# Two-layer convolution and sparse-coding kernel: the normalisation statistics go through TensorE once instead of twice, and the work is put in another order

## The reference

```python
def _gn(v, G=32, eps=1e-5):            # two channels form a group
    g = v.reshape(B_, G, C_ // G, H_, W_)
    m = jnp.mean(g, axis=(2, 3, 4), keepdims=True)
    s = jnp.var(g, axis=(2, 3, 4), keepdims=True)
    return ((g - m) / jnp.sqrt(s + eps)).reshape(v.shape)

x = x + _L0_conv_ref(_gn(x), L0_conv_weight)       # 3 x 3 convolution, circular
x = x + _L1_conv_ref(_gn(x), L1_conv_dictionary)   # sparse coding of 4 x 4 patches
```

## Time and profile before

| | us |
|---|---|
| median of 3 runs | 3585.17 |
| lowest, highest | 3581.29, 3589.22 |
| profiled execution | 3581.48 |
| its span (first to last instruction) | 3579.5 |
| PE busy | 3067.3 (86%) |
| DVE busy | 2579.2 (72%) |
| ACT busy | 2367.6 (66%) |
| POOL busy | 1856.7 (52%) |

### The profile page before, as it was taken

The page is one execution under the profiler, slowest core; times in us unless marked ns, Lnnn a source line. Parts: engine busy times, 40 slices in busy tenths (PEclk is TensorE's granted clock), DMA queues, the critical chain, the costliest instruction groups (busy, mean ns, idle before and its releaser), DMA issues.

```text
span 3579.5 us, 35041 instructions
## 1 busy us (share of the span) xinstructions
PE 3067.3 (86%) x9488; PEld 1310.8 (37%) x9488; DVE 2579.2 (72%) x6596; ACT 2367.6 (66%) x3795; POOL 1856.7 (52%) x1861
## 2 busy tenths in 40 slices
PE   6796889899898989989898989989898998986617
PEld 2232333343333334333333434333333433332303
DVE  2027887878788687878778786878778777887872
ACT  3535686858677676858668685767768576765634
POOL 0015565555555564655656555555655555556651
PEclk8998999999999989999999999999999999997858
DMA  3433443534354343434444353445435344442222
GB/s 114 154 108 117 136 132 97 180 84 145 102 163 132 124 139 91 156 91 154 133 141 131 101 177 73 151 114 158 127 109 163 86 144 102 127 106 60 59 59 47
DMA packets 131028, 428.38 MB, mean 120 GB/s; under 512 B 55696, under 2 KB 55952, under 8 KB 106128
## 3 DMA queue, kind: packets, MB, share of 16 engines
q0 software_dynamic: 91136, 202.10, 23.3%
q1 hardware_dynamic: 39696, 224.05, 17.1%
HBM read 289.70 MB, written 136.31 MB: 119 GB/s over the span
## 4 chain that ended last, share of the span: by engine, by line
PE 49%; DVE 15%; issue 10%; ACT 10%; POOL 8%; DMA 5%; ACTq 0%; POOLq 0%; SPq 0%; DVEq 0%
PE gen_ps L909 22%; PE gen_ps L918 15%; PE conv_ps L952 8%; POOL v L479 7%; DVE u L832 6%; ACT hot L543 4%; PE conv_ps L959 4%; DMA u<-marked_rows,chosen 4%; DVE idx L732 2%; DVE h L840 2%; DVE top L723 2%; ACT score L617 1%; ACT junk_sums L356 1%; ACT ct L530 1%; ACT z L567 1%
## 5 line engine op out<-in xcount | busy, mean ns | idle before, releaser
L479 POOL DMA_INDIRECT v<-gram_rows,cell x1280 | 1278.2, 999 | 919.3 <-DVE cell L741 392.4
L909 PE MATMUL gen_ps<-ct,dt 128*128 128x512 f32 x2048 | 948.1, 618 | 69.6 <-ACT rb L555 60.3
L918 PE MATMUL gen_ps<-dn,z 128*128 128x512 f32 x2048 | 927.9, 607 | 62.4 <-ACT z L567 50.8
L952 PE MATMUL conv_ps<-xh,wc 128*128 128x512 f32 x1536 | 717.1, 617 | 91.0 <-ACT xa L585 83.5
L491 POOL DMA_INDIRECT u<-marked_rows,chosen x504 | 506.1, 1004 | 492.8 <-DVE chosen L737 329.0
L723 DVE MAX8 top<-score 128x8 f32<-128x512 f32 x640 | 420.7, 691 | 294.6 <-ACT score L617 278.5
L909 PEld LDWEIGHTS gen_ps<-ct,dt 128*128 128x128 f32 x2048 | 400.5, 198 | 583.2 <-issue 571.2
L918 PEld LDWEIGHTS gen_ps<-dn,z 128*128 128x128 f32 x2048 | 389.9, 194 | 568.0 <-issue 512.9
L832 DVE SCALAR_TENSOR_TENSOR u<-u,nl 128x512 f32<-128x512 f32 x748 | 514.2, 747 | 95.4 <-DMA u<-marked_rows,chosen 92.6
L617 ACT ACTIVATE score<-h 128x512 f32<-128x512 f32 x640 | 377.6, 604 | 241.3 <-DVE h L840 120.4
L655 DVE SCALAR_TENSOR_TENSOR ce<-hot,xc,ce 128x512 f32<-128x512 f16 x512 | 365.1, 745 | 159.1 <-ACT hot L546 159.1
(11 more groups left out here) (103 smaller groups left out, 1870.5 us busy)
## 6 DMA issues: line engine op xcount, KB each, us to landing
xh<-x_paired SPq DMA_DIRECT2D x128, 650.0 KB, 4.0
xa<-x_pairs SPq DMA_DIRECT2D x64, 1024.0 KB, 6.1
y_rows<-xa SPq DMA_DIRECT2D x64, 1024.0 KB, 6.3
y_rows<-rb POOLq DMA_DIRECT2D x64, 1024.0 KB, 8.3
v<-gram_rows,cell POOLq DMA_INDIRECT x1280
u<-marked_rows,chosen POOLq DMA_INDIRECT x504, 3.8
dn<-atoms SPq DMA_DIRECT2D x1, 2048.0 KB, 7.8
gram_rows<-u SPq DMA_DIRECT2D x4, 256.0 KB, 2.0
```

The lines of the kernel that those rows point to most:

```text
L479: pool.indirect_dma_start(v[:, g, k - 1, j, t:t + 1], None, cells, bass.IndirectOffsetOnAxis(ap=cell[:, g, k // (KMAX - 1), j, t:t + 1], a ...
L909: last = pe.matmul(to[:], dt_[:, a, d, :], ct[:, a, :], start=(a == 0), stop=(a == NA - 1))
L918: last = pe.matmul(to[:], z[:, t % 2, d // PATCH, d % PATCH, :], dn[:, d, :], start=(d == 0), stop=(d == ND - 1))
L952: pe.matmul(conv_ps[:, a], wc[:, tap, a * CIN:a * CIN + P], rows[:, a + 1:a + 2 * CP:2, tap:tap + W], start=(tap == 0), stop=False)
```

## The change

1. The average is one product. `mv` gets three more columns, the partition's mean times +1 or -1 in three sign patterns over the four partitions (made by ACT, a new instruction). PE averages all five columns in one product. The sum of the squares of the three signed averages equals the variance of the four means, so `spread` and the two DVE instructions before it go. ACT squares and adds the three (with an accumulator), adds the averaged variance, and takes the root with eps as its bias: three ACT instructions in a row in `root`. DVE keeps five instructions instead of nine.
2. DVE's pieces stand in other places: `gn 1` whole at place 30, `gn 0` at 37.5; `co 1` goes from 23.5 to 24 and `co 0` from 1.5 to 0.5.
3. ACT's list is new, PE's list is new in the second half of the period, so is `BANKS`; on POOL the second addition to the output goes from unit 5 to unit 6. The tables of the tail change in the same way: there, two pairs of coefficient tiles stand at other units (13 instead of 17.5, 27 instead of 22.5, 33 instead of 27).

```diff
-GN_STEPS = 10
-GN_SUMS = (3, 2)
+GN_STEPS = 5
+GN_SUMS = (2, 1)
+GN_ROOT = 3
 VECTOR_PLAN = {
-    1.5: [("co", 0)], 3: [("ce", 0, 0)], 10.5: [("ce", 0, 1)], 23.5: [("co", 1)], 24: [("ce", 1, 0)],
-    30: [("ce", 1, 1), ("gn", 1, 1)], 31: [("gn", 1, 2), ("gn", 1, 3)], 37: [("gn", 0, 1)],
-    39.5: [("gn", 0, 2), ("gn", 0, 3), ("gn", 0, 4)],
+    0.5: [("co", 0)], 3: [("ce", 0, 0)], 10: [("ce", 0, 1)], 24: [("co", 1), ("ce", 1, 0)],
+    30: [("ce", 1, 1), ("gn", 1, 1)], 37.5: [("gn", 0, 1)], 39.5: [("gn", 0, 2)],
 }
 SCALAR_PLAN = {
...
+    11: [("oh", 0, 3, 2), ("oh", 0, 2, 3), ("oh", 0, 3, 3), ("oh", 0, 2, 4), ("oh", 0, 3, 4), ("ct", 0, 1),
+        ("ev", 3), ("z", 6), ("oh", 1, 0, 1), ("st", 10), ("st", 11), ("z", 7), ("oh", 1, 1, 1), ("oh", 1, 0, 2)],
...
 ADD_PLAN = {
-    4: [(0, 0)], 5: [(0, 1)], 7: [(1, 0)], 9: [(1, 1)],
+    4: [(0, 0)], 6: [(0, 1)], 7: [(1, 0)], 9: [(1, 1)],
 }
...
+                act.activation(mv[:, n, 2:5], avg[:, P:], ACT.Copy, scale=mv[:, n, 0:1]).then_inc(gn_ready[n], 1)
...
             def root(image, n):
-                act.wait_ge(gn_step[n], at(image, GN_STEPS, 5))
-                act.activation(gsc[n][:, 4:5], gsc[n][:, 3:4], ACT.Sqrt).then_inc(gn_root[n], 1)
+                gs = gsc[n]
+                act.wait_ge(gn_sum[n], at(image, GN_SUMS[n], 1))
+                act.activation(gs[:, 6:9], st_ps[:, 5 * n + 2:5 * n + 5], ACT.Square, accum_out=gs[:, 0:1]).then_inc(gn_root[n], 1)
+                act.wait_ge(gn_root[n], at(image, GN_ROOT, 1))
+                act.activation(gs[:, 1:2], st_ps[:, 5 * n + 1:5 * n + 2], ACT.Identity, bias=gs[:, 0:1]).then_inc(gn_root[n], 1)
+                act.wait_ge(gn_root[n], at(image, GN_ROOT, 2))
+                act.activation(gs[:, 2:3], gs[:, 1:2], ACT.Sqrt, bias=eps[:, 0:1]).then_inc(gn_root[n], 1)
...
-                    dve.wait_ge(gn_sum[n], at(i, GN_SUMS[n], 1))
-                    dve.tensor_copy(gs[:, 0:1], st_ps[:, 3 * n:3 * n + 1]).then_inc(gn_step[n], 1)
+                    dve.wait_ge(gn_root[n], at(i, GN_ROOT, GN_ROOT))
+                    dve.reciprocal(gs[:, 3:4], gs[:, 2:3]).then_inc(gn_step[n], 1)
...
-            def spread(i, n):
-
-                pe.wait_ge(gn_step[n], at(i, GN_STEPS, 4))
-                pe.matmul(st_ps[:, 3 * n + 1:3 * n + 2], avg[:], gsc[n][:, 2:3], start=True, stop=True).then_inc(gn_sum[n], 1)
+                pe.wait_ge(gn_ready[n], at(i, 2, 2))
+                pe.matmul(st_ps[:, 5 * n:5 * n + 5], avg[:, 0:P], mv[:, n, :], start=True, stop=True).then_inc(gn_sum[n], 1)
```

93 lines of the change are left out of this document (39 added, 54 removed), and 108 rows, old and new, of tables (BANKS, SCALAR_PLAN, TAIL_SCALAR_PLAN, TAIL_VECTOR_PLAN).

## The result

The changed kernel takes 3617.26 us (median of 3 runs, 3614.91 to 3618.56) where the kernel before takes 3585.17: ratio 1.0088, interval 1.0071 to 1.0105. It is slower, by 32 us; 3558 was predicted and 3603 was the end of the range.

What follows compares the result with a forecast made beforehand. A chain through DVE, ACT and POOL bounds each period up to tile 6's transposes, then PE. Gains of 21 (periods), 3 (start) and 2 (tail), 26 us, gave 3555.5 profiled, put at 3558; 8-in-10 range 3510 to 3603.

Steps and rivals of the forecast that it cites:

- Steps 1 to 4: Full period: first coefficient pair 1.4 us earlier, unit 3 rows 58.9, round 4's hole about 0.2, correlation 7 2.6 us ahead.
- two table loads: On ACT: no loads beyond the two; the rival, two more per root, gave 3660 us, chance 0.02.
- cheap squares: ACT's three added instructions: about 1 us per normalisation, 2 per period, taken as free except where on the path.
- half rate that I feared behind correlation 7's hole: After correlation 7's 2.8 us hole: half clock would lose 1.7 us, making the period 205.2 instead of 203.5.
- Step 5: Second half of the coefficients: round 6 ends at 96.3, one-hot rows at 111.2, pair at 112.0, 2.1 us ahead.
- Step 6: Last coefficient pair ends at 142.5, transpose for tile 6 starts at 141.3, reconstruction at 145.4, 1.0 us ahead.
- Step 7's premise: Rest of the period after tile 6's transpose: the same products, 55.9 us, and the same 2.2 lost to half rate.
- Start and tail: Outside the full periods: 3 us gained at start and early periods (0 to 6), 2 in the tail (9 gained to 6 lost).
- mine for "slower": Rival: path through ACT's list in steps 4 to 6, 1.5 us a period longer, 3605 us; chance 0.23.

Runs made afterwards that it cites:

- experiment 3: Changed kernel with all plans, banks and TensorE's order of the kernel before, so the new statistics alone: ratio 1.0005 to the kernel before.
- experiment 4: Changed kernel with convolution round 7 put back behind reconstruction 4: ratios 1.0004 and 1.0017 to the kernel before; the changed kernel beside it 1.0108.
- experiment 7: Copies of reconstructions 4 to 7 wait for no addition: changed kernel 1.0031, kernel before with early round 7 1.0306, kernel before 0.9991.

## Why the prediction was wrong

Steps 1 to 4 came out, in both periods looked at: round 4 without a hole (at 49.3 us), round 5 after a hole of 0.6 and 1.1 (1.4 said), correlation 7 at 76.6 and 77.1 behind a wait of 2.39 for `h` (77.7 and 2.8 said). The two table loads and the cheap squares were right: the statistics cost nothing (experiment 3), and the average waits for nothing.

The half rate that I feared behind correlation 7's hole worked the other way round. It came in three of the twelve periods, and these are the short ones: round 6, and so SyncE's loads, come 1.0 us later there. My reading that a hole of 2.82 led to it every time was too strong: in one of the 13 full periods of the kernel before, round 4 comes after the same 2.82 and runs at the full clock. TensorE there, and the stretch by engine:

```profile
2267.08 5.40 PE L952 MATMUL conv_ps<-xh,wc 128*128 128x512 f32 x12 [2.82 <-ACT xa L585]
```

```profile
2266.00:2274.00 8.00, 6.92 (x28) 2.85 (x32) 3.69 (x20) 7.57 (x15) 4.62 (x5) 1.00 0.79 269
```

Step 5 came out in the short period (last one-hot 110.8, pair 111.6; 111.2 and 112.0 said), not in the long one (pair 113.8, about where it was). It booked the earlier end of round 6 as a gain and did not ask what starts there: the loads that make POOL's sixteenth gather land late.

Step 6 failed in all periods. It put the last pair's end at 142.5 and the transpose for tile 6 at 141.3. The pair ended at 145.2 in the short period and 150.2 in the long one, and the transpose came at 147.3 on average, 143.8 in the short period and 148.9 in the long one. I walked ScalarE's row with "the old durations", and two of them were not durations of ScalarE: the copy of reconstruction 4 waits for the landing of an addition, and unit 4's last scores wait for gathers. Steps 1 to 5 had moved round 7, and so the evacuation that SyncE waits for, 14 us forward. I counted its products and its copy, but not the two 1 MB stores that it issues, and never asked what they would then run beside. On the first chip they ran beside the addition, which took 11.2 us instead of 7.8, and in nine of twelve periods beside unit 4's last two gathers. In the three periods in which those gathers were all issued ahead of the stores, ScalarE's copy waited 3.4 to 4.0 us for the addition, and yet the period was no longer than before. All of the 38 us are in the nine others.

What is shown, and where: on the late chips the early round 7 is what costs (experiment 4), and in the full periods it costs through the landing (experiment 7). On the first chip the packets show that the addition stood behind the stores: its first packet comes 1.6 us after its issue in the kernel before, and 5.8 to 6.0 in the long periods, when the stores' last packets end, 5.5 to 6.5 after it. That the loads behind round 6 and the late gathers make the nine periods long is read from their going together in twelve of twelve periods; no run on that chip took one of them away, and how much of the loss is round 7's there stays open.

Step 7's premise (the same products after transpose 6) was right to 0.7 us: 61.5 for 62.2. POOL's second addition no longer waits ahead of gathers, but now runs after them, which gained nothing since VectorE was the later one.

Start and tail: 5 us were expected. The start and the early periods lost 4.4 net with the first full one left out (-0.9 - 4.0 + 9.3), because I checked bank 2 for the two correlations in a full period only, not in image 1's, where nothing lies between them. The tail gained 3.7 where 2 was said.

The rivals: mine for "slower" had the place roughly (ScalarE's list up to the last pair), but another mechanism and 1.5 us a period; 3.2 were lost. None had a transfer in it.

## What to carry to other kernels

When a step is moved, forward above all, list the transfers whose issue waits for it, and look in the trace at what they will then run beside and who waits for those to land. In an engine's row, a copy into a single buffer is as late as the transfer that empties it, and so is everything behind it: find these gates first and keep work that only fills time behind them. Compare every period before calling a wait the cause: here the clearest wait on one chip, 4 us at the gate, stood in the periods that lost nothing. Check a new bank or buffer assignment also in the first and last turns of a loop, where the work that separates two users is missing.
